# A stream chunk gathered and an output chunk scattered by GpSimd, by row numbers, in a hybrid convolution, expert and attention kernel

## What is computed

```python
x = L0_attn_a_u
x = x + _L0_attn_a_ref(_layernorm(x), ...)   # long convolution by FFT, kernel K from A_log, C_re, log_dt, plus u * D
x = x + _L0_ffn_ref(_layernorm(x), ...)      # 8 experts, top 2, hidden 256, relu
x = x + _L0_attn_b_ref(_layernorm(x), ...)   # causal attention, 16 heads, 4 query sets
x = x + _L0_ffn_ref(_layernorm(x), ...)      # the same experts again
```

## Time and profile before

| | us |
|---|---|
| time, median of 2 runs | 806.01 (804.57 to 807.45) |
| span of the profiled execution | 802.7 |
| PE busy | 760.7 (95%) |
| ACT busy | 721.1 (90%) |
| DVE busy | 652.5 (81%) |
| POOL busy | 560.4 (70%) |

### The profile page before, as it was taken

The page is one execution under the profiler, slowest core; times in us unless marked ns, Lnnn a source line. Parts: engine busy times, 40 slices in busy tenths (PEclk is TensorE's granted clock), DMA queues, the critical chain, the costliest instruction groups (busy, mean ns, idle before and its releaser), DMA issues.

```text
span 802.7 us, 20426 instructions
## 1 busy us (share of the span) xinstructions
PE 760.7 (95%) x7674; PEld 414.0 (52%) x7674; DVE 652.5 (81%) x1917; ACT 721.1 (90%) x932; POOL 560.4 (70%) x685
## 2 busy tenths in 40 slices
PE   5888999999999999999999999999989999999996
PEld 4345666677775333333333333333334777677774
DVE  7998999999876677778787777787566898989885
ACT  5918999999999999999999999999997999899984
POOL 2898665655436988888988888888896545445442
PEclk9999999999999999999999999999999999999998
DMA  9210000000044343443453334424400000000000
GB/s 276 67 64 29 1 2 2 2 2 2 8 100 106 80 93 88 98 83 90 105 107 96 90 91 90 98 67 106 107 1 2 1 15 16 15 14 16 15 15 18
DMA packets 37962, 45.70 MB, mean 57 GB/s; under 512 B 6137, under 2 KB 23810, under 8 KB 37858
## 3 DMA queue, kind: packets, MB, share of 16 engines
q1 hardware_dynamic: 37858, 44.33, 22.2%
HBM read 27.53 MB, written 16.78 MB: 55 GB/s over the span
## 4 chain that ended last, share of the span: by engine, by line
PE 54%; ACT 19%; DVE 14%; issue 11%; POOL 1%; DMA 0%; ACTq 0%; DVEq 0%; POOLq 0%
PE psum L1006 13%; ACT prob L1272 13%; PE psum L937 13%; PE psum L1316 12%; PE psum L1263 5%; DVE mixed L1025 4%; PE psum L1374 4%; ACT hidden_first L951 2%; ACT hidden_parts_first L953 2%; PE psum L1154 1%; PE psum L686 1%; DVE hidden_parts_first L960 1%; DVE hidden_parts_second L960 1%; DVE stats L362 1%; PE psum L646 1%
## 5 line engine op out<-in xcount | busy, mean ns | idle before, releaser
L1272 ACT ACTIVATE prob<-psum 128x1536 f32<-128x1536 f32 x256 | 347.6, 1499 | 14.4 <-PE psum L1263 14.4
L1279 POOL TENSOR_SCALAR_AFFINE_SELECT prob<-prob 128x512 f32<-128x512 f32 (+3 forms) x448 | 305.9, 712 | 41.1 <-ACT prob L1272 31.7
L1316 PE MATMUL psum<-prob,vstack 128*32 128x256 f32 (+1 forms) x2048 | 204.9, 495 | 1.6 <-DVE o_tok L1324 1.6
L937 PE MATMUL psum<-xt_parts,w_parts 128*128 128x512 f16 x768 | 186.6, 379 | 0.0
L1025 DVE SCALAR_TENSOR_TENSOR mixed<-psum,comb_y,mixed 128x128 f32<-128x128 f32 x512 | 143.2, 340 | 1.5 <-PE psum L1006 1.5
L967 POOL TENSOR_TENSOR hidden_parts_second<-hidden_second,hidden_parts_second 128x512 f16<-128x512 f32 x64 | 77.4, 1209 | 93.5 <-ACT hidden_parts_second L953 93.5
L967 POOL TENSOR_TENSOR hidden_parts_first<-hidden_first,hidden_parts_first 128x512 f16<-128x512 f32 x64 | 77.6, 1213 | 78.1 <-ACT hidden_parts_first L953 78.1
L1263 PE MATMUL psum<-qstack,kstack 32*128 32x512 f16 x768 | 99.7, 385 | 9.2 <-ACT prob L1272 7.8
L1263 PEld LDWEIGHTS psum<-qstack,kstack 32*128 32x128 f16 x768 | 24.9, 91 | 157.3 <-ACT prob L1272 138.7
L937 PEld LDWEIGHTS psum<-xt_parts,w_parts 128*128 128x128 f16 x768 | 71.2, 98 | 64.1 <-issue 1.4
L951 ACT ACTIVATE hidden_second<-psum,b 128x512 f32<-128x512 f32 x128 | 88.4, 691 | 15.4 <-PE psum L937 12.0
(11 more groups left out here) (148 smaller groups left out, 848.4 us busy)
## 6 DMA issues: line engine op xcount, KB each, us to landing
qstack<-qk_parts SPq DMA_DIRECT2D x128, 128.0 KB, 3.5
qk_parts<-parts SPq DMA_DIRECT2D x64, 192.0 KB, 3.1
kstack<-qk_parts SPq DMA_DIRECT2D x128, 32.0 KB, 3.5
stream<-u_folded SPq DMA_DIRECT2D x4, 512.0 KB, 8.1
kept_x<-stream SPq DMA_DIRECT2D x4, 512.0 KB, 2.6
out<-mixed SPq DMA_DIRECT2D x7, 256.0 KB, 2.3
w_whole<-L_ffn_W SPq DMA_DIRECT2D x1, 1024.0 KB, 9.0
taps<-c_taps SPq DMA_DIRECT2D x1, 640.0 KB, 7.1
```

The costliest lines, as they stand in the source:

```text
L937: last = e.matmul(bank(u % 4), m.w1[:, w_part, ex, cols], xt_parts[:, s, x_part, :], start=(n == 0), stop=(n == len(PRODUCTS) - 1))
L1272: e.activation(prob[:, n % PROBS, :], psum[:, TILE * (n % 2):TILE * (n % 2 + 1)], ACT.Exp, scale=SCALE)\
L1279: return e.affine_select(kept, kept, [[0, kept.shape[1]], [0, 2], [sign, P]], ALU.is_ge, 0.0, base=0, channel_multiplier=-sign)
L1316: last = e.matmul(to[SLOT * lane:SLOT * (lane + 1)], vstack[:, b % 2, keys, first:first + SLOT], weights_of(n - t, lane, keys, pair), star ...
```

## The change

Row numbers 0 to 4095 come to the chip as a constant of 128 x 32 unsigned integers (`c_rows`, tile `row_no`); number t * 128 + p in partition p, column t is the row of the stream's tile t that partition p holds.

The fourth chunk of the stream isn't loaded by SP any more. GpSimd gathers it, after `weight` is zeroed, in eight indirect transfers of one tile each (128 rows of 512 bytes), each adding 16 to `s_x[3]`, for which VectorE now waits as 8 x 16. Output chunk 5 (the sixth of eight) isn't stored by SP; GpSimd scatters it in four indirect transfers of one tile each, behind its cut of expert 3 of chunk 6, once `accum` tells that chunk 5 is summed up. SP's last wait and the general path wait for these four too.

```diff
@@ build_in @@
+    row_no = sb("row_no", [P, TILES], U32)
@@ vector_conv_stats @@
-        e.wait_ge(s_x[ch], 16)
+        e.wait_ge(s_x[ch], 16 * (CONV_TILES if ch + 1 == CONV_CHUNKS else 1))
@@ sync_loads @@
         load_x(0)
+        e.dma_start(row_no[:], dr["c_rows"]).then_inc(s_rows, 16)
         e.dma_start(eye[:], dr["c_eye"]).then_inc(s_small, 16)
...
         e.dma_start(w2_whole[:], w2_rows).then_inc(s_w2, 16)
-        load_x(3)
         e.dma_start(wg[:], dr["L0_ffn_Wg"]).then_inc(s_expw, 16)
@@ new @@
+    def gpsimd_gather_last(e):
+        e.wait_ge(s_rows, 16)
+        for t in range(TILES - CONV_TILES, TILES):
+            e.indirect_dma_start(stream[:, t, :], None, x_rows, bass.IndirectOffsetOnAxis(row_no[:, t:t + 1], 0))\
+             .then_inc(s_x[CONV_CHUNKS - 1], 16)
+
+    SCATTERED = FFN_CHUNKS - 3
+
+    def gpsimd_scatter_chunk(e):
+        e.wait_ge(accum, EXPERTS * (second.at + SCATTERED + 1))
+        for t in range(SCATTERED * FFN_TILES, (SCATTERED + 1) * FFN_TILES):
+            e.indirect_dma_start(out_rows, bass.IndirectOffsetOnAxis(row_no[:, t:t + 1], 0), mixed[:, t, :], None)\
+             .then_inc(s_scattered, 16)
@@ gpsimd_second @@
                 gpsimd_low(e, second, ch, ex)
+                if (ch, ex) == (SCATTERED + 1, 3):
+                    gpsimd_scatter_chunk(e)
@@ sync_program @@
         for ch in range(FFN_CHUNKS - 1):
-            sync_store(e, second, ch, s_stored)
+            if ch != SCATTERED:
+                sync_store(e, second, ch, s_stored)
...
         e.wait_ge(s_stored, STORED)
+        e.wait_ge(s_scattered, 16 * FFN_TILES)
@@ gpsimd_program @@
         gpsimd_taps(e)
+        gpsimd_gather_last(e)
         gpsimd_conv(e)
```

More of the change, by code:

```diff
@@ L124, in shape_constants @@
         "c_eye": np.eye(P, dtype=np.float32),
+        "c_rows": np.arange(TILES * P, dtype=np.uint32).reshape(TILES, P).T.copy(),
         "c_masked": np.where(position[None, None, :] <= position.reshape(HALVES, P).T[:, :, None], 0.0, MASKED)
@@ L265, in build_in @@
     out_tiles = out.rearrange("b (h p) m -> p (b h) m", p=P)
+    x_rows = dr["u_folded"].rearrange("b t m -> (b t) m")
+    out_rows = out.rearrange("b t m -> (b t) m")
     w1_rows = dr["L0_ffn_W1"].rearrange("e d h -> d e h")
@@ L274, in build_in @@
     s_x = [sem(f"landed_x{i}") for i in range(CONV_CHUNKS)]
+    s_rows = sem("landed_row_numbers")
+    s_scattered = sem("scattered_rows")
     s_kept, s_stored = sem("kept_x_stored"), sem("out_stored")
@@ L1746, in gpsimd_second @@
                     gpsimd_route(e, second, ch + 1, routing_step(ch + 1, ex))
-    STORED = 16 * (FFN_CHUNKS + 1)
+    STORED = 16 * FFN_CHUNKS
     def sync_store_last(e):
```

## The result

| | before | after |
|---|---|---|
| median of the runs | 806.01 us (804.57 to 807.45) | 811.43 us (810.57 to 812.29) |
| ratio | | 1.0077, 95% interval 1.005 to 1.0105 |
| span of the profiled execution | 802.7 us | 810.6 us |
| GpSimd's first `rstd` | 12.07 us | 16.96 us |
| ScalarE's first `normed` | 14.78 us | 20.78 us |

The changed kernel is slower by 0.8%, inside the predicted range. Two executions far outside the others, one of the kernel before (867.97 us, granted clock 0.85) and one of the half gathers (1863.35 us, at full clock, cause unknown), count in no ratio.

The account below looks back on a forecast made before the run. PE (95% busy) was taken as the bound, with GpSimd's added work deciding the cost: start 8.5, clock 0.4, scatters 1.1, together 10.0 us on the 802.7 span, 812.7; with the median 3.3 above, 816.0 us, range 808.5 to 825.

Parts of the forecast that it names:

- What bounds the start: Convolution's start: first `offset` has 0.5 us of slack before `normed` at 14.78; lateness beyond it isn't won back.
- SP's queue: SP's loads at the start: later issues move forward by up to 4.7 us, row numbers land at 5.9; cost 0.
- g: Duration of one gather on GpSimd: taken as 1.2 us, a software loop over 128 rows, bounds 0.20 and 1.66.
- L: What two configuration commands start ahead of GpSimd's first `rstd`: taken as 5.5 us, bounds 0 and 10.1.
- rival 1: Load behind the configuration commands short or hidden: `normed` 3.0 us late, total cost 4.1, time 810; chance 0.25.
- the forecast: Main case for the whole kernel: g from 1.0 to 1.6, L from 3 to 8, time 811 to 822; chance 0.50.
- The start's sum: Convolution's start: `rstd` at 5.9 + 9.6 + 5.5 = 21.0, `normed` at 23.26 instead of 14.78, 8.5 us late.
- TensorE's clock: First forward transforms: PE idles some 7 us, then runs at a low clock; cost 0 to 1.2, put at 0.4 us.
- The scatters: Second expert layer, chunk 6: the cut of expert 4 queues behind four scatters; PE stalls once, 4g - 3.75 = 1.1 us.
- The median: Whole kernel: median of the runs taken as 3.3 us above the profiled span of 802.7, with a spread of 2.9.
- Rival 2: Gathers at the start over 2 us each from full DMA rings: at 2.4 us, 825.6, slower by over 2%; chance 0.15.
- Rival 3: No change: gathers at 0.5 us and L below 2 end before 12.07, scatters within slack; time 806; chance 0.10.

Follow-up runs that it names:

- the half gathers: Eight gathers of 64 rows each, SyncE loading the other 64 partitions in one transfer, no scatters, against the kernel before: 808.77 against 804.52 us, ratio 1.0044.
- The repeated execution: The changed kernel, unedited, in more executions against the kernel before: 810.87 against 804.66 us, ratio 1.0077; its profile had no late increment.
- the profile on record: First profiled execution of the changed kernel, span 810.6 us, with late TensorE increments; that kernel's median was 811.43 against 806.01 us before.
- the three others: Three later profiled executions of the unedited changed kernel, without late increments: first `up` at 62.89, 62.83 and 63.02 us.

## Why the prediction was right, and where its sizes were not

**What bounds the start: right.** The half microsecond of slack ahead of the first `normed` decided. The chain of the repeated execution goes through the gathers, `rstd`, `offset` and `normed`, and the lateness of 4.45 at `normed` is 4.47 at the first `up`: nothing is won back, as said. So the half microsecond and the path were right.

**SP's queue: cost 0, as said, but not by the way described.** The issues behind the removed load hardly moved forward: the next one, `wg`, took the wait in its place, in the profile on record 5.44 us at 12.42 where the load had taken 4.74 at 11.59. SP reaches the last of these issues at 20.54, against 20.80 before. The row numbers were there at 6.0 (5.9 predicted).

**g, one gather: nearly right, for the wrong reason.** I took 1.2 us as a loop over 128 rows; the period is 1.24, plus 1.1 for the first two together. The last ended at 16.8, not 15.5. That the period met 1.2 is luck: no row of before told it. With half the rows it stays at 0.90, so it is no loop over rows, and the price would have been wrong for any other number of them.

**L, what the configuration commands start: this is the step that failed.** I took 5.5 us, the middle of 0 and 10.1. The repeated execution has 0.11 us between the last gather and `rstd` (0.07 for the two commands and 0.04). The mechanism of rival 1 held, with its condition L near 0, to which I had given 0.25; the forecast with L from 3 to 8 had 0.50 and did not come. The range held all the same, since it took in rival 1. Rival 1's 810 is near 810.87 only because its errors cancel: the start was 1.45 and the scatters 0.3 too low, the median 1.35 too high. The Trainium skill (GPSIMD Engine Reference, Instruction dispatch) puts some 6 us on the first call after new code is loaded; no run here shows it at this place, and the measurement decides.

**The start's sum.** 8.5 became 4.45: 5.4 too much for L, 1.3 too little for the gathers and the row numbers. Also, with its own upper bounds (g 1.6, L 8) the forecast reaches 823, not the 822 that I wrote. In the profile on record it was 6.0, since there the held increment of `tap_rows` was later than GpSimd. The prediction had no step for that; without it the span would have been about 809, as the three others show. Its cause is open.

**TensorE's clock: 0.4 became 0.** The slow stretch came: TensorE stood 3.3 us ahead of the first transforms, and in the repeated execution its windows show the granted clock at 0.50 and 0.69 of full speed, about the lower level of 1.2 GHz (window, busy us, clock, DMA share, GB/s):

```profile
24.00:26.00 2.00, 2.00 (x3) 0.50 0.06 24
26.00:28.00 2.00, 2.00 (x4) 0.69 0.00 0
```

Eight transforms took 5.37 us instead of 3.60, and VectorE waited 0.44 for them; but the chain runs by `stats`, `vareps` and GpSimd's `rstd` of chunk 2 there, which need no matmul. The wait was of the size that I had named, on a branch that does not end last. It is also not an additional slow stretch but the one of before, moved: there the eight transforms from 25.37 took 5.37 us, here those from 23.29, and those from 29.83 on ran at a granted clock of 1.00.

**The scatters: right, 1.1 became 1.44.** The rule, four periods less 3.75, gives with 5.05 us for the four and 1.15 for the cut 1.3; one stall only, at the place named. The second effect that I had not costed is the three cuts then queued back to back: VectorE's own cut, begun in the midst of them, took 3.42 us instead of 0.67 in the repeated execution and ended 0.55 us behind GpSimd's last.

```profile
771.08 3.38 POOL L987 TENSOR_TENSOR hidden_parts_second<-hidden_second,hidden_parts_second 128x512 f16<-128x512 f32 x3
```

```profile
771.59 3.42 DVE L980 TENSOR_TENSOR hidden_parts_second<-hidden_second,hidden_parts_second 128x512 f16<-128x512 f32 x1 [0.63 <-ACT hidden_parts_second L973]
```

The Trainium skill (SBUF — State Buffer, Who interferes with whom) says that a VectorE instruction with two inputs in SBUF contends with a GpSimd instruction that reads SBUF, and calls the contention an exclusive lock; the 3.42 agrees. Here it was hidden.

**The median.** I put it 3.3 us above the profiled span, from two runs of before that lay 2.9 apart. In 27 runs it was 804.66, that is 2.0 above the span of 802.7. That was 1.35 too much in my 816. With the measured terms the sum is 816.0 - 4.05 - 0.4 + 0.3 - 1.35 = 810.5, against 810.87 in six executions.

**The rivals.** Rival 2 (2 us a gather from full queues) is out: the gathers kept their 0.94 while the DMA engines' busy share was 1.09 from 8 to 16 us. The other reason given with it, that VectorE makes gathers long, was nearer than I thought: beside `powers` the second gather took 1.78 us, and that the first two are not 0.94 is 1.1 of the 4.45 us. It met two of the eight, not all, and by an instruction with two inputs in SBUF. Rival 3 (no change) would have needed 0.5 us a gather; eight plain transfers came at 0.56, all but in this time, and did just that.

## What to carry to other kernels

Count the indirect transfers on GpSimd as instructions of 1.25 us each, hardly less with half the rows (here 64 or 128), add what is left of a long two-input VectorE instruction that is under way when one begins, and lay them where that engine waits anyway: four fitted into the wait ahead of the first `rstd` at no cost, eight did not; one between two cuts was free, four in a row cost 1.44 us. Where an engine has half a microsecond of slack ahead of the chain, whatever is put in front of it beyond that is paid in full at the end. Before taking the middle of a wide bound for a hidden cost, ask which rows exclude the rest; and take the base from more than two runs if they lie as far apart as the effect.

## What the runs showed of the hardware that I had not expected

- A gather or scatter by row numbers holds GpSimd 0.94 to 0.96 us and 0.30 more to the next, for 128 rows (0.90 for 64), where VectorE is not in its way; a plain transfer of the same tile 0.56 in all.
- One that begins while VectorE is in a TENSOR_TENSOR with two inputs in SBUF takes what is left of that plus 0.82 to 0.86 us: 1.7 to 1.8 for the second gather beside `powers`, 1.39 and 1.33 for two scatters in a row beside VectorE's cuts, 1.24 and 1.25 for two laid between GpSimd's cuts (eighteen cases). Eight plain transfers beside the same `powers` were not lengthened.
- The first indirect transfer of a program takes 0.1 to 0.3 us more besides (a first scatter 1.20 us, against 1.10 for the same one with gathers ahead; a first gather the remainder plus 1.02 to 1.11). Why is open, and so is why the first scatter of a row takes 1.10 us and not 0.96 with gathers ahead.
- In one of twelve profiled executions with indirect transfers nine of TensorE's 1107 increments came 0.6 to 6.0 us late, all while such transfers went out, and about half of the records of these transfers' landings are missing there. It cost 1.5 us at the start and nothing at the scatters. It wasn't found again, and its cause is open.
